# A counting sort in a graph kernel: column counts on TensorE, first places through DRAM and a triangle product in place of 49 scans

## What is computed

```python
# layer 0
agg = jnp.zeros_like(x).at[src].add(edge_attr)        # 100,000 rows into 6,250
h = relu(concat([h, agg, attention], 1) @ W1.T + b1) @ W2.T + b2
# layer 1
ht = relu(h @ W1 + b1)
msg = sigmoid(w * ht[src] + b_param)
fsum = segment_sum(msg, dst, num_segments=6250)
c = (log(s / (1 - s)) - b_param) / w                   # s = clip(fsum)
out = relu(normalize(concat([ht, c], 1) @ Wn + bn))
```

## Time and profile before

| | us |
|---|---|
| median of three runs | 2751.17 |
| lowest and highest | 2750.54, 2754.43 |
| span of the profiled execution, first to last instruction | 2749.1 |
| first stage, to the end of the last scatter | 426.4 |
| first tile stage | 429.7 to 1272.8 |
| fold and dense part | 1272.8 to 1549.9 |
| second tile stage | 1549.9 to 2569.2 |
| last stage | 2569.2 to 2749.1 |

### The profile page before, as it was taken

The page is one execution under the profiler, slowest core; times in us unless marked ns, Lnnn a source line. Parts: engine busy times, 40 slices in busy tenths (PEclk is TensorE's granted clock), DMA queues, the critical chain, the costliest instruction groups (busy, mean ns, idle before and its releaser), DMA issues.

```text
span 2749.1 us, 37581 instructions
## 1 busy us (share of the span) xinstructions
PE 1967.5 (72%) x9329; PEld 1367.5 (50%) x9329; DVE 2030.7 (74%) x6057; ACT 1332.7 (48%) x4292; POOL 1805.9 (66%) x1687
## 2 busy tenths in 40 slices
PE   1459994667777777778977566777777777776785
PEld 0347773454354354355765445535535535544474
DVE  2685545787987997997774588799799799753586
ACT  0124444445645645645235444564564564564554
POOL 1477777777777777773022477777777777777246
PEclk9669995799999999999998768899999899986898
DMA  9888878635633333332656533333333333333243
GB/s 383 243 173 185 186 142 218 151 98 134 152 101 102 104 98 102 102 98 70 219 185 221 167 102 100 104 101 98 102 103 97 102 103 97 103 105 105 81 138 109
DMA packets 181579, 370.26 MB, mean 135 GB/s; under 512 B 32281, under 2 KB 100659, under 8 KB 178818
## 3 DMA queue, kind: packets, MB, share of 16 engines
q0 software_dynamic: 93168, 219.39, 31.7%
q1 hardware_dynamic: 77010, 113.58, 12.9%
q10 hardware_dynamic: 11200, 35.00, 3.3%
HBM read 281.48 MB, written 99.46 MB: 139 GB/s over the span
## 4 chain that ended last, share of the span: by engine, by line
DVE 36%; PE 24%; issue 13%; POOL 9%; DMA 8%; SPq 3%; ACT 3%; DVEq 2%; ACTq 0%; POOLq 0%
PE bank L1392 22%; DVE agg L1155 16%; POOL store L649 7%; DMA store<-g_table,idx_all 4%; DVE oh L1087 3%; DVE hits L1083 3%; DVE cum L1012 3%; DVE cum L1042 2%; DVE store L1079 2%; DMA store<-in_edge_attr,idx_all 2%; DVEq L1147 2%; SPq L451 1%; DVE msk L905 1%; ACT store L717 1%; DVE store L905 1%
## 5 line engine op out<-in xcount | busy, mean ns | idle before, releaser
L1392 PE MATMUL bank<-store,oh 128*128 (+1 forms) x6770 | 1448.5, 360 | 537.5 <-DVE agg L1155 139.2
L1392 PEld LDWEIGHTS bank<-store,oh 128*128 128x128 f32 (+1 forms) x6770 | 941.8, 165 | 1020.0 <-issue 457.4
L1155 DVE TENSOR_TENSOR agg<-bank,agg 128x256 f32 x1845 | 769.0, 417 | 319.9 <-PE bank L1392 242.1
L649 POOL DMA_INDIRECT store<-g_table,idx_all x785 | 778.0, 991 | 255.4 <-issue 168.1
L789 ACT ACTIVATE oh<-dist 128x128 f32<-128x128 f32 x1845 | 534.5, 304 | 821.8 <-PE bank L1392 791.8
L649 POOL DMA_INDIRECT store<-in_edge_attr,idx_all x628 | 635.1, 1011 | 195.0 <-issue 132.8
L781 ACT ACTIVATE dist<-iota,nloc_all 128x128 f32<-128x128 f32 x1845 | 582.6, 386 | 68.9 <-DVE nloc_all L1127 68.1
L623 POOL DMA_INDIRECT agg_copy<-agg x160 | 255.4, 1596 | 165.8 <-ACT agg L744 73.3
L1087 DVE TENSOR_TENSOR oh<-hits,v 125x512 f16<-125x512 f16 x720 | 285.7, 420 | 7.3 <-DVE nmr L993 0.2
L1079 DVE TENSOR_TENSOR store<-iota,ttab 125x628 f16<-125x628 f16 x360 | 172.0, 478 | 71.1 <-PE bank L1392 70.5
L1392 PE MATMUL bank<-agg 128*128 128x256 f32 (+2 forms) x480 | 125.5, 416 | 101.3 <-issue 55.9
(11 more groups left out here) (196 smaller groups left out, 1467.7 us busy)
## 6 DMA issues: line engine op xcount, KB each, us to landing
agg_copy<-store ACTq DMA_DIRECT2D x4, 6400.0 KB, 35.8
agg<-in_edge_attr SPq DMA_DIRECT2D x39, 512.0 KB, 5.1
store<-in_x SPq DMA_DIRECT2D x72, 256.0 KB, 4.8
agg_copy<-agg_copy POOLq DMA_DIRECT2D x16, 800.0 KB, 7.1
store<-g_table,idx_all POOLq DMA_INDIRECT x785
store<-in_edge_attr,idx_all POOLq DMA_INDIRECT x628
pre_scratch<-store SPq DMA_DIRECT2D x25, 256.0 KB, 5.3
agg<-agg_copy SPq DMA_DIRECT2D x25, 256.0 KB, 7.9
```

Of the source, the lines that this page charges most:

```text
L649: gp.indirect_dma_start(out=store[:, at % RING * D:(at % RING + 1) * D], out_offset=None, in_=table_dram, in_offset=bass.IndirectOffsetOnA ...
L1155: dve.tensor_tensor(to, pt[n % TB][:, 0:D], to, ALU.add).wait_op(s_mm, n + 1, "sem-ge").then_inc(s_acc, 1)
L1392: return pe.matmul(o, l, r, start=start, stop=stop, skip_group_check=skip)
```

## The change

Masks are made for seven ranges at a time by one comparison with a table of numbers. TensorE counts the edges of each column and range: 160 matmuls, with the column's 49 masks as weights and one column of ones. From the counts (49 rows, 160 columns) VectorE makes each column's first place in its range, as a high and a low f16 part (`brow`). SyncE stores them to DRAM and loads them back as two rows below the masks (partitions 125 and 126 of `msk`). One product of the masks with these two rows and a triangle of ones (`tri16`) gives every place, three ranges at a time, 17 products of up to 480 columns; VectorE multiplies each by the mask and writes the 16-bit places. The scans, `cnt` and `adj` are gone. Atoms and their weights change with that, and so the steps in which all later atoms stand. Some semaphores of the attention are merged, and one weight's transpose goes to another PSUM bank.

```diff
-SCAN_ATOM = SEGS
-COUNT_ATOM = SCAN_ATOM + -(-NWS // SLOTW)
-PLACE_ATOM = COUNT_ATOM + 2
-SLOT_ATOM = PLACE_ATOM + 9
-TREE_ATOM = SLOT_ATOM + -(-NWS // SLOTW)
+COUNT_ATOM = SEGS
+COUNTS = 8
+CC_ATOM = COUNT_ATOM + COUNTS
+PLACE_ATOM = CC_ATOM + 5
+PRE_ATOM = PLACE_ATOM + 13
+PW = 3
+PRES = -(-NWS // PW)
+TREE_ATOM = PRE_ATOM + PRES
...
         def job_weight(a):
-            if a < SCAN_ATOM:
-                return 0.75
-            if a < COUNT_ATOM:
-                return 0.8
-            if SLOT_ATOM <= a < TREE_ATOM:
-                return 0.75
+            if a < CC_ATOM:
+                return 0.7
+            if PRE_ATOM <= a < TREE_ATOM:
+                return 0.65
             if a < RANK_ATOMS:
-                return 0.6 if TREE_ATOM <= a < SPLIT_ATOM else 0.25
+                return 0.6 if TREE_ATOM <= a < SPLIT_ATOM else 0.35
...
+            def column_starts(sig):
+                sp.wait_ge(s_start, sig + 1)
+                sp.dma_start(brow_dram.rearrange("r (w c) -> w r c", w=NWS),
+                             brow.rearrange("w (r c) -> w r c", r=2)).then_inc(s_startd, 16)
+                sp.wait_ge(s_startd, 16 * (sig + 1))
+                sp.dma_start(msk[KP:KP + 2, :], brow_dram[:, :]).then_inc(s_startl, 16)
...
             for b in range(EBLKS):
+                if b == starts_block:
+                    column_starts(0)
...
-                if n < SCAN_ATOM:
-                    for w in range(n * WSEG, (n + 1) * WSEG):
-                        do(ts(m3[:, w, :], win[K, cols], float(w), None, ALU.is_equal))
-                elif n < COUNT_ATOM:
-                    for w in range((n - SCAN_ATOM) * SLOTW, min((n - SCAN_ATOM) * SLOTW + SLOTW, NWS)):
-                        do(dve.tensor_tensor_scan(c3[:, w, :], m3[:, w, :], m3[:, w, :], 0.0, ALU.add, ALU.max))
-                elif n == COUNT_ATOM:
-                    dve.tensor_copy(cnt[K, :], c3[:, :, COLS - 1]).then_inc(s_cnt, 1)
+                if n < COUNT_ATOM:
+                    w0 = n * WSEG
+                    r = dve.tensor_tensor(m3[:, w0:w0 + WSEG, :].rearrange("p w (f i) -> p w f i", i=2),
+                                          win[K, cols].rearrange("p (f i) -> p f i", i=2).unsqueeze(1).to_broadcast([KP, WSEG, COLS // 2, 2]),
+                                          iota2[K, w0:w0 + WSEG, :].unsqueeze(2).to_broadcast([KP, WSEG, COLS // 2, 2]), ALU.is_equal)
...
+                elif n == CC_ATOM:
+                    dve.wait_ge(s_cc, sig + 1)
+                    do(dve.tensor_copy(colcnt, pS[0:NWS, 0:COLS]))
+                elif n == CC_ATOM + 1:
+                    do(dve.tensor_tensor_scan(colend, colcnt, colcnt, 0.0, ALU.add, ALU.max))
...
                 elif n < TREE_ATOM:
-                    for w in range((n - SLOT_ATOM) * SLOTW, min((n - SLOT_ATOM) * SLOTW + SLOTW, NWS)):
-                        do(dve.scalar_tensor_tensor(out=p3[:, w, :], in0=c3[:, w, :], scalar=adj[K, w:w + 1],
-                                                    in1=m3[:, w, :], op0=ALU.add, op1=ALU.mult))
+                    i = n - PRE_ATOM
+                    w0, w1 = i * PW, min(i * PW + PW, NWS)
+                    dve.wait_ge(s_pf, sig * PRES + i + 1)
+                    dve.tensor_tensor(cum[K, w0 * COLS:w1 * COLS].bitcast(I16), (pS, pR)[i % 2][K, 0:(w1 - w0) * COLS],
+                                      msk[K, w0 * COLS:w1 * COLS], ALU.mult).then_inc(s_pfd, 1)
...
+            def column_counts(sig, part):
+                if part == 0:
+                    pe.wait_ge(s_mask, sig + 1)
+                masks = msk[K, :].rearrange("p (w f) -> p w f", w=NWS)
+                for c in range(part * COLS // COUNTS, (part + 1) * COLS // COUNTS):
+                    r = mm(pS[0:NWS, c:c + 1], masks[:, :, c], ones16[K, 0:1], True, True)
+                if part == COUNTS - 1:
+                    r.then_inc(s_cc, 1)
...
+            def prefix(sig, i):
+                w0, w1 = i * PW, min(i * PW + PW, NWS)
+                if i == 0:
+                    pe.wait_ge(s_startl, 16 * (sig + 1))
+                elif i >= 2:
+                    pe.wait_ge(s_pfd, sig * PRES + i - 1)
+                mm((pS, pR)[i % 2][K, 0:(w1 - w0) * COLS], tri16[0:KP + 2, 0:KP], msk[0:KP + 2, w0 * COLS:w1 * COLS], True, True
+                   ).then_inc(s_pf, 1)
```

More of the change, by code:

```diff
@@ L268, in gnn_program @@
         part_a = cum[:, 0:2 * SORTS * COLS].bitcast(I32)
+        cumf = cum[:, :].bitcast(F32)
+        colcnt, colend, colstart = (cumf[0:NWS, n * COLS:(n + 1) * COLS] for n in range(3))
+        diag = cumf[0:NWS, 3 * COLS:3 * COLS + NWS]
+        brow = cum[0:NWS, 8 * COLS:10 * COLS]
         v2i = v2[:, :].bitcast(I16)
@@ L487, in x_norm @@
                 x_rows(n)
+            def column_starts(sig):
[4 more added lines that the diff above has]
+                sp.dma_start(msk[KP:KP + 2, :], brow_dram[:, :]).then_inc(s_startl, 16)
+            starts_block = next(b for b in range(EBLKS) if PLACE_ATOM + 3 in BLOCKS[b])
             def pre_store(n):
@@ L513, in _ @@
                                  aggc_dram[0].rearrange("(c j p) f -> c p j f", p=P, j=2)[n]).then_inc(s_zf[r], 16)
+            for sig in range(1, G1 + 1):
+                column_starts(sig)
             sp.wait_ge(s_a1, 2 + NW)
@@ L569, in _ @@
             streamed(x1_load, y0_g_store)
+            for sig in range(G1 + 1, SORTS):
+                column_starts(sig)
             sp.wait_ge(s_mm, len(ORDER))
```

114 lines of the change are left out of this document (74 added, 40 removed).

## The result

The changed kernel takes **2810.39 us** (median of 4 runs, 2802.91 to 2812.89); the kernel before, on the same chip, 2752.8 us. The ratio is 1.0208, 95% interval 1.0192 to 1.0224: **58 us slower**, where the prediction had 22 us faster and a range that ends at 2754 us. The profiled execution of the changed kernel has a span of 2807.1 us.

What follows compares the result with a forecast made beforehand. GpSimd's gathers were taken to pace 1,862 of the 2,749 us. From 2749.1, less 14 (first stage) and 8 (tile stages), came 2727.1, with 2.1 around it 2729 us; range 2710 to 2754 us.

Steps and rivals of the forecast that it cites:

- ring: Tile stages: 20 gathers issued ahead, letting TensorE and VectorE be some 25 us behind before GpSimd waits.
- Tile stages: 8 us less: Both tile stages: 3 us of gather waits go and shorter gathers give 5 us; range 0 to 16 us.
- VectorE's work: Per sort: masks of 745 ns, products of 657 ns, 25 us less in all, 226 us over nine sorts.
- The count, 0.08 us: TensorE, each one-column count matmul: 0.08 us, 12.8 us per sort, allowed from 0.03 to 0.2 us.
- rival B: Tile stages, six groups: counts at 0.2 us, above a 0.14 us threshold, make GpSimd wait 60 us; 2789 us, chance 0.09.
- TensorE has 96 jobs at 0.49 us: A group's first 48 steps, two jobs each (double steps): with 17 us of new work, TensorE needs 64 us.
- A lag of 15 us at most: A group's first 48 steps: work falls at most 15 us behind the gathers, so GpSimd never waits.
- Masks: 0.5 us per group: Tile stages: the new masks, as f16 work on VectorE, lengthen the gathers by 0.5 us per group.
- The trip through DRAM hidden: Tile stages: SyncE's store and reload lies behind ten atoms, 6 to 7 us; hidden, or a wait up to 3 us.
- First stage, 14 us: Stage before the first gather: 11.9 us from VectorE plus 4.4 us from TensorE, minus 2.3 us, 14 us less.
- Coefficients: 11.9 us forecast: First stage, end of VectorE's block 12: the layer norm's coefficients come 11.9 us earlier, from savings after 92 us.
- A: Gathers hide all; x loads, later edge loads or TensorE's clock hold the first stage: 2747 or 2751 us, chance 0.14.

Runs made afterwards that it cites:

- a_pick_ts: a_pick with the kernel before's 49 single-input masks in place of the 7 new two-input masks: 2732.94 us, ratio 0.9926.
- a_pick: The changed kernel with the same counts got by 49 accumulating products of 160 columns instead of 160 of one column: 2742.85 us, ratio 0.9959.
- a_wide128: The changed kernel with 128 equal columns of ones instead of one in each count, the further columns unused: 2759.97 us, ratio 1.0039.
- the fills: Three unread 512-column products added per x chunk of the first stage: a_pick_ts 0.9896 to 0.9926, changed kernel 1.0186, kernel before 0.9964 and 0.9962.

## Why the prediction was wrong, point by point

- **What bounds the kernel**: right. Gathers pace the tile stages, a ring of about 25 us stands between them and TensorE, and the waits at the places at which it runs dry grew by 56 us of the 58.
- **"Tile stages: 8 us less"**, for VectorE's lighter work: too small. In the changed kernel it is hidden behind the new waits and masks; a_pick_ts, which has neither, shows it. Its tile stages, to be held against the earlier trace rows:

```profile
430.10:1262.50 832.40, 615.35 (x3158) 442.14 (x3158) 630.06 (x1835) 427.17 (x1530) 641.37 (x644) 0.88 0.45 124
1539.90:2551.80 1011.90, 743.13 (x3568) 523.87 (x3568) 717.35 (x2041) 545.12 (x1951) 773.09 (x785) 0.88 0.36 103
```

  They are 11 and 7 us shorter. GpSimd's own busy time fell by 15 us, and the 3 us of waits are gone. I had the waits right and put the shorter gathers at 5 us. 7 of the 15 us lie in the first group, whose gathers took 1.031 us before, longer than in the groups of the earlier trace rows, and which my sum leaves out.
- **VectorE's work**: right (masks 0.732 us for 0.745, products 0.649 for 0.657, 203 us in all for 226).
- **The count, 0.08 us**: 0.090 to 0.092 us, inside the range. From start to start a pick product with its weights side by side takes the same, 0.088 us. The weight loads by themselves differ, here in the changed kernel (320 bytes apart) and in a_pick (side by side), by form:

```profile
L1441 PEld LDWEIGHTS bank<-ones,msk 125*49 125x49 f16 x1440 | 127.6, 177 | 59.6 <-issue 36.1 <-DVE msk L1037 23.5
L1442 PEld LDWEIGHTS bank<-msk,pick 125*49 125x49 f16 x441 | 33.3, 112 | 49.4 <-DVE msk L1038 26.8 <-issue 22.4
```

  A load of 49 spread weights is recorded with 0.177 us on average, one of 49 side by side with 0.112, and the spread loads fill 127.6 of the 133.5 us of their products. So they may be what sets the 0.090 us, but rival B's 0.2 us was far off. The Trainium skill, page "SBUF — State Buffer", section "Door 1: The DMA port swizzle", has accesses that cross into a new 16-byte line pay each time, and stood beside rival B. The longer loads agree with it in direction; no run here tells that rule from another cause, since the pick products differ in their columns too.
- **"TensorE has 96 jobs at 0.49 us": this is the step that failed.** I took the price of a job at the clock of the rows and carried it into a stretch which my own change fills with one-column products. At full clock a job takes 0.53 us; beside the counts, where 0.50 of the clock was granted, it takes 1.0 us. No term of the sum and no rival let the price of the *old* work depend on the new. a_wide128 prices this at 47 us: 16 jobs of a group at about 0.5 us too much are 8 us, six times.
- **"A lag of 15 us at most"**: failed as well, by less. Even at full clock eight steps take 2.9 us (1.84 + 1.07) and not 1.25: 13 us from them alone, on top of what was there. In a_wide128 the ring just ran dry at the counts (waits of 0.07 us over the usual), and then where triangle products and jobs make VectorE's step 1.45 us. I had compared 60 us of work with 60 us of time over all 48 steps; what counts is the worst run of steps within them. From a_wide128 to a_pick 22 us (0.8%) come back. Of these the traces place 12 us, the gathers' waits that are left in a_wide128; where the rest lies they don't show.
- **Masks: 0.5 us per group** was 1.5 us, and from a_pick to a_pick_ts 0.33% or 9 us. I had taken the rate of the column batches and the masks' own 5 us of work; the trace shows 24 gathers lengthened. The Trainium skill, page "SBUF — State Buffer", section "Who interferes with whom", has a VectorE instruction with two inputs in SBUF contend with GpSimd's reads, and one with at most one such input not, outside its two-port modes. By that rule the trace agrees on three counts: gathers of 1.05 us beside the new masks, 0.946 beside the old, and 0.945 us (11.34/12, the third window of gathers above) where the products from PSUM lie.
- **The trip through DRAM hidden**: right (a_pick).
- **First stage, 14 us**: it was -1 us. Coefficients: 11.9 us forecast, 4.2 measured. I had counted all of VectorE's savings from 92 us on. But up to 112.5 us, where block 6 begins in both kernels, 19.95 us of work became 11.62 us and nothing came earlier: the waits for x and for the sums (3.92 and 2.08 us, above) took the place. The windows of VectorE alone, before:

```profile
92.00:112.50 20.50, 19.95 (x73) 0.67 0.96 265
```

and after:

```profile
92.00:112.50 20.50, 11.62 (x53) 0.50 0.95 260
```

  From the coefficients to the first gather I forecast 2.1 us less and it was 5.1 us more (243.2 against 238.1), although 5.5 batches fewer lie in it. Of the 7.2 us between, 6 go to the clock by the windows from 200 to 400 us ((44 - 32)/2). With the clock held up by the fills on both sides the changed first stage is at most 6 us ahead (413.7 to 416.7 against 416.4 to 420.1 us).
- **The rivals**: B had the right place and the right symptom, gathers waiting behind the double steps, at a chance of 0.09, but for a wrong reason: its threshold of 0.14 us per count was never reached. A was right for the first stage, its doubt about the clock and the x loads included.

In parts, against the kernel before, in the order in which the runs took them away: clock in the tile stages +47, bare time of the counts +22, new masks +9 us. Without these three the version a_pick_ts stands at -20 us, 18 of them in the tile stages.

## What to carry to other kernels

Before adding many narrow products, ask what they do to the work that stands between them: price the old work again at the lower clock, and look at whether the same result can be had from few wide products (here 49 of 160 columns for 160 of one). Compare work and time over the worst run of steps that the buffer must carry, not over the whole phase. And time taken off an engine counts only from behind the last wait for something else.

## What the runs showed of the hardware that I had not expected

- In the count stretch TensorE's timeline shows no pause, 20 us of 20 are busy, and yet 1.2 GHz was granted (0.50) with counts of one column and with counts of 16; with 128 it was 2.4 GHz (1.00). The Trainium skill, page "TensorE: Matmul & The Clock Gate", section "HAM oscillation — how this bites in real kernels", tells of a clock that falls in pauses of TensorE. These rows show a fall without one.
- A product with 49 weight columns took 0.090 us from start to start with 1 column at 1.2 GHz, and 0.092 and 0.088 us with 128 and 160 columns at 2.4 GHz. Its weight load was recorded with 0.177 us where the 49 weights lie 320 bytes apart (changed kernel) and with 0.112 us side by side (a_pick).
- A stretch that TensorE bounds can be shortened by *more* work in it: 75 products of 512 columns brought the first gather 10 to 16 us forward, 25 did nothing, and 125 gave part of it back. The clock of that stretch rose with it, from 0.89 to 0.97 and from 0.92 to 0.98.
- Chips differ: the same kernel took 2751 us on some and 3007 to 3036 us on others, with the same length of a gather (0.945 us) in the group without a sort, and a kernel 0.4% faster there may not be so elsewhere.
